# Zeroing the diagonal blocks of a decay attention's probabilities on GpSimd instead of adding a mask on TensorE

## What is computed

```python
scores = einsum('bhqd,bhkd->bhqk', q, k) / sqrt(8)
scores = where(causal, scores, -inf)
w = softmax(scores, axis=-1)
w = w * decay_weight_matrix(T)          # 1 near the diagonal, falling to 0
ctx = einsum('bhqk,bhkd->bhqd', w, v)
```

## Time and profile before

| | us |
|---|---|
| median of three runs | 5766.71 |
| lowest, highest | 5761.96, 5769.86 |
| the profiled execution, its own time | 5796.54 |
| its span | 5794.8 |
| first and last decay product on GpSimd (line 966) | start at 921.8 and 1410.1 |

### The profile page before, as it was taken

How to read it: one execution, slowest core, us unless ns; L and a number is a source line. 1 busy time by engine, 2 the same in 40 slices (tenths; PEclk the granted TensorE clock), 3 DMA queues, 4 the chain that set the end, 5 groups by cost and what they waited for, 6 DMA issues and landing times. The chain is left out here.

```text
span 5794.8 us, 91401 instructions
## 1 busy us (share of the span) xinstructions
PE 4718.3 (81%) x33501; PEld 2088.3 (36%) x33596; DVE 3782.7 (65%) x4596; ACT 3159.8 (55%) x6002; POOL 1685.3 (29%) x1468
## 2 busy tenths in 40 slices
PE   5677667998679977799766998589877799699999
PEld 2233223443233335333352333256432344233344
DVE  6899657886589943899437992577638710699410
ACT  5666444676448852488524885434466521388621
POOL 0666315885032324322242221000006400123100
PEclk7899888999889988899887999789989999799999
DMA  0000011111021124211242110000000000111100
GB/s 27 0 1 1 4 42 41 42 44 28 10 71 51 51 86 148 71 50 51 83 142 73 49 50 20 6 10 2 5 10 0 20 0 0 37 31 45 42 0 14
DMA packets 132106, 211.55 MB, mean 37 GB/s; under 512 B 36422, under 2 KB 93619, under 8 KB 130293
## 3 DMA queue, kind: packets, MB, share of 16 engines
q1 hardware_dynamic: 126708, 197.74, 11.3%
q0 software_dynamic: 4992, 8.41, 0.5%
HBM read 153.93 MB, written 52.00 MB: 36 GB/s over the span
## 5 line engine op out<-in xcount | busy, mean ns | idle before, releaser
L947 ACT ACTIVATE l_core_probs<-l_core_ps_scores_b 128x512 f32<-128x512 f32 (+3 forms) x3840 | 1610.7, 508 | 581.0 <-PE l_core_ps_scores_b L863 426.2
L1047 DVE TENSOR_REDUCE l_core_chunk_max<-l_core_ps_scores_a 128x2 f32<-128x1024 f32 (+3 forms) x1280 | 1253.7, 1021 | 82.9 <-PE l_core_ps_scores_a L848 47.8
L863 PE MATMUL l_core_ps_scores_b<-l_q_rows_sb,l_k_rows_sb 64*128 64x512 bf16 (+3 forms) x3840 | 944.0, 332 | 32.5 <-ACT l_core_probs L947 10.1
L848 PE MATMUL l_core_ps_scores_a<-l_k_rows_sb,l_q_rows_sb 64*128 64x512 bf16 (+3 forms) x3840 | 741.4, 346 | 163.9 <-DVE l_core_ps_acc L1005 75.9
L996 POOL TENSOR_SCALAR_AFFINE_SELECT l_core_probs<-l_core_probs 128x512 f32<-128x512 f32 x512 | 326.9, 639 | 1169.9 <-ACT l_core_probs L947 1165.7
L878 PE MATMUL l_core_ps_acc<-l_core_probs,l_v 128*9 128x512 f32 (+3 forms) x6144 | 648.9, 494 | 15.9 <-ACT l_core_out_sums L929 9.1
L1047 DVE TENSOR_REDUCE l_core_neg_max<-l_core_ps_scores_a 128x2 f32<-128x256 f32 (+3 forms) x640 | 493.6, 820 | 97.6 <-PE l_core_ps_scores_a L808 96.0
L863 PEld LDWEIGHTS l_core_ps_scores_b<-l_q_rows_sb,l_k_rows_sb 64*128 64x128 bf16 x3840 | 304.4, 94 | 689.9 <-ACT l_core_probs L947 600.4
L1918 POOL TENSOR_TENSOR l_scan_bx<-l_xs,l_scan_b_rows 128x1024 f32<-128x1024 f32 x192 | 452.5, 2357 | 224.1 <-DVE l_scan_states L1928 217.8
L1928 DVE TENSOR_TENSOR_SCAN l_scan_states<-l_scan_ps_decay,l_scan_bx 128x1024 f32<-128x1024 f32 x192 | 439.8, 2290 | 40.7 <-POOL l_scan_bx L1918 15.3
L966 POOL TENSOR_TENSOR l_core_probs_decayed<-l_core_probs,l_decay 128x1536 f32<-128x1536 f32 (+2 forms) x160 | 394.2, 2488 | 156.5 <-ACT l_core_probs L947 156.5
(11 more groups left out here) (323 smaller groups left out, 7683.4 us busy)
## 6 DMA issues: line engine op xcount, KB each, us to landing
l_slots_weights<-m_both_dram SPq DMA_DIRECT2D x78, 512.0 KB
l_q_rows<-l_proj_parts SPq DMA_DIRECT2D x96, 128.0 KB
l_k_rows<-l_proj_parts SPq DMA_DIRECT2D x96, 128.0 KB
l_q_rows_sb<-l_q_rows SPq DMA_DIRECT2D x128, 96.0 KB
l_k_rows_sb<-l_k_rows SPq DMA_DIRECT2D x128, 96.0 KB
l_heads_out<-l_core_out_sums SPq DMA_DIRECT2D x300, 32.0 KB
l_q_rows_sb<-l_q_rows SPq DMA_DIRECT2D x128, 64.0 KB
l_k_rows_sb<-l_k_rows SPq DMA_DIRECT2D x128, 64.0 KB
```

The costliest lines, as they stand in the source:

```text
L848: mm = nc.tensor.matmul(slot[:, i, 0:w], qs[n % 3][rows, p, qt * P:(qt + 1) * P], ks[n % 3][rows, p, c * NT:c * NT + w], start=True, stop= ...
L863: mm = nc.tensor.matmul(pb[m % 3][:, 0:w], ks[n % 3][rows, p, kt * P:(kt + 1) * P], qs[n % 3][rows, p, q0:q0 + w], start=True, stop=not diag)
L947: nc.scalar.activation(pt[:, ts % RP, j, 0:w], pb[m % 3][:, 0:w], ACT.Exp, scale=scale).then_inc(b_free, 1)
L1047: nc.vector.tensor_reduce(to, pa[e % 2][:, :, 0:width_a(qt, c)], AX.X, ALU.max, negate=True).then_inc(a_free, 1)
```

## The change

In the decay attention the second scores lose their mask products. Instead GpSimd runs the same `affine_select` as in the other layers on the four heads' diagonal blocks of `probs` (128 partitions by 4 x 128), ahead of the decay product of the same step, and the decay product waits for its end (`cut`). `values` on TensorE now waits for `cut` in this layer too. `PLAN_DECAY` is another string with the same counts. All else, the other attention layers too, stays.

```diff
-PLAN_DECAY = ("bbbvbaa", "bbvbba", "bvbabba", "babbb", "bbabavbaa", "bbvabba",
-              "bvbabbav", "bbabvab", "bbvabba", "bavbbbaav", "bbabab", "bvbbbaa")
+PLAN_DECAY = ("bbbvb", "bavbababa", "bvbbba", "bbabba", "babbvaab", "bbvbbaa",
+              "bbvbaba", "bvbbavb", "babvbb", "babbvb", "bbvbaaaaab", "bvbbbaaa")
...
-                    diag = decay and q0 == kt * P
...
-                    mm = nc.tensor.matmul(pb[m % 3][:, 0:w], ks[n % 3][rows, p, kt * P:(kt + 1) * P],
-                                          qs[n % 3][rows, p, q0:q0 + w], start=True, stop=not diag)
-                    if diag:
-                        mm = masked(pb[m % 3][:, 0:P], i, maskk, (slice(0, 64), slice(0, P)))
-                    mm.then_inc(b_ready, 1)
+                    nc.tensor.matmul(pb[m % 3][:, 0:w], ks[n % 3][rows, p, kt * P:(kt + 1) * P],
+                                     qs[n % 3][rows, p, q0:q0 + w], start=True, stop=True).then_inc(b_ready, 1)
...
-                    if not decay and on_diag(c, kt):
+                    if on_diag(c, kt):
                         pe.wait_ge(cut, had_diag(ts))
...
+                def cut_diagonal(ts):
+                    pool.wait_ge(b_free, 4 * ts + 4)
+                    block_ = pt[:, ts % RP, :, 0:P]
+                    nc.gpsimd.affine_select(block_, block_, [[0, 4], [1, P]], ALU.is_ge, none, base=0,
+                                            channel_multiplier=-1).then_inc(cut, 1)
+
                 if decay:
                     pool.wait_ge(c_in, CIN)
                     for ts in range(NS_ * GROUPS):
                         c, kt = STEPS[ts % NS_]
                         wd, off = decayed(c, kt), first_q(c, kt) - kt * P
+                        if on_diag(c, kt):
+                            cut_diagonal(ts)
+                            pool.wait_ge(cut, had_diag(ts))
                         if wd:
```

More of the change, by code:

```diff
@@ L956, in _ @@
             def _(pool):
+                none = nc.gpsimd.to_reg(0.0)
+                def cut_diagonal(ts):
[3 more added lines that the diff above has]
+                                            channel_multiplier=-1).then_inc(cut, 1)
                 if decay:
@@ L969, in _ @@
                 else:
-                    none = nc.gpsimd.to_reg(0.0)
                     def max_parts(n):
@@ L993, in _ @@
                         if on_diag(*STEPS[t]):
-                            pool.wait_ge(b_free, 4 * ts + 4)
-                            block_ = pt[:, ts % RP, :, 0:P]
-                            nc.gpsimd.affine_select(block_, block_, [[0, 4], [1, P]], ALU.is_ge, none, base=0,
-                                                    channel_multiplier=-1).then_inc(cut, 1)
+                            cut_diagonal(ts)
                         if t == 8 and n + 1 < GROUPS:
```

## The result

| | before | after |
|---|---|---|
| median of four runs, us | 5768.28 | 5873.31 |
| lowest, highest | 5761.96, 5771.29 | 5866.35, 5876.28 |
| the profiled execution's own time | 5796.54 | 5873.84 |
| one group of the decay core | 30.08 | 37.14 |

The ratio is 1.0182, with an interval of 1.0164 to 1.0199: the change makes the kernel 105 us slower. The stage itself accounts for it. From the first decay product to the end of the last `values` it runs from 921.77 to 1412.3 us before and from 921.73 to 1514.1 after, 101.8 us more. The 14 periods from the first step 7 to the fifteenth are 94.9 us of that (422.5 before, 517.4 after): most groups are 7.06 us longer, a few less. The remaining 7 us lie ahead of the first step 7 (2.4), between the last two (1.7) and at the end (2.7). I had said 5798, 5826 at most.

The account below looks back on a forecast made before the run. TensorE with its hand-overs set the pace before; after, a GpSimd loop of 32.15 us a group against 30.08 would: +29 over 14 periods, -1 as backlog drains, +2.8 at the end, together +31, 5798 us; range 5772 to 5826.

Parts of the forecast that it names:

- The direction: Whole kernel: slower by 31 us; slower given 81%, faster by more than 0.2% given 4%.
- the added work: GpSimd, decay core: eight selects a group at 0.70 us with hand-over, 5.6 us, raising its work from 24.47 to 30.1.
- the loop: GpSimd, step 3's `values`, ScalarE's copy, step 7: 28.8 + 3.35 = 32.15 us a group, +29 over 14 periods; 60%.
- the way back: From the end of step 3's decay product to step 7's start, through `values`, copy of `acc` and exponentials: 3.35 us.
- The end: Last five GpSimd products, alone on the path: four of these steps gain a select, +2.8 us.
- The term ahead of it: From the fifteenth step 7 to the last: GpSimd's backlog drains and the masks give back 1 us, -1.
- The price of the masks: TensorE's removed mask products in the second scores: 1.4 to 2 us a group, 22 to 32 if TensorE set the pace.
- VectorE's 26.63 fits too: VectorE's busy time of 26.63 us a group was taken to fit within the 32.15 us period.
- the order as a mere rival: The later turning of the maxima under the new plan was counted only in the shared-port rival, 17%, 5826 us.
- The second rival: Shared port and later turning: VectorE held for a GpSimd product, step 10 late 2 us; period 34.2, +59, 5826; 17%.
- The clock: TensorE's clock falls from waiting between steps 1 and 3, perhaps 2 us a group on the path: 5830; 5%.

Follow-up runs that it names:

- e1: The kernel after with the PLAN_DECAY order of before (selects, no mask products): 5837.36 us against 5797.98 before, ratio 1.0067, 32.43 us a group.
- e9: The kernel after with first-score units set where they stood before, second scores and `values` in the new order: 5802.37 us against 5764.12, 32.41 a group.
- e4: The kernel after with the old order and no selects, diagonal blocks left unmasked: 5788.79 us against 5797.98 before, ratio 0.9983, 29.49 a group.
- e12b: The kernel after with fourteen filler products on TensorE where its 4 us wait stands: 5859.89 us against 5765.00 before, 35.0 and 36.6 a group.
- e3: The kernel after with the remainder of VectorE's split of the maxima kept in PSUM: 5847.17 us against 5797.98 before, 32.13 or 33.7 a group.
- e11: The kernel before with the new order, masks kept, no selects, split remainder in PSUM: 5821.90 us against 5764.12 before, 33.15 or 34.8 a group.
- e6: The kernel before with only the split remainder moved to PSUM: 5772.89 us against 5764.12 before, ratio 1.0011, 30.08 us a group.
- e2: The kernel before with the new order alone, masks kept, no selects: 5890.60 us against 5797.98 before, ratio 1.0150, 35.9 to 37.1 a group.

## Why the prediction was wrong

**The direction and the added work were right.** Selects take 0.64 us, the hand-over to the product 0.07 to 0.08, and GpSimd's work a group rose to 29.5 (30.1 forecast, 29.6 without hand-over). GpSimd cannot take it in, for the reason given: e1 has the loop at 32.43 against 32.15. By itself this term gives e9's +38 us, where I had +31. In the kernel after the way back is 3.34 against 3.35, but that agreement is in part luck. One wait in it I had not named: step 6's product waits 0.64 us for the `values` of step 3, that is for a buffer. And I took 3.35 instead of 3.75 because one more unit of step 7 stands ahead. e9 has that unit ahead too, and its way back is 3.65 (1000.65 to 1004.30); the last 0.3 came with the new places of the first-score units.

**The end was right.** From step 7's product of the last group to the last product's end pass 16.76 us after (1496.68 to 1513.44) and 14.10 before: 2.66 more, 2.8 forecast. The term ahead of it was not: from the fifteenth step 7 to the last I had -1 us, since the backlog would drain; measured are 38.41 us after and 36.71 before, +1.7.

**The price of the masks was too high**, 0.59 us a group measured by e4 and 1.4 to 2 forecast from the earlier trace rows. I priced TensorE's rate where TensorE is only one of the engines that pass the work around. It did not matter for the sum, which GpSimd's loop set. Two small slips did not matter either: the lower bounds of my terms add up to 31.0 us, not 31.3, and ahead of step 10 stand two selects, not three (10.55 us behind step 7, where I wrote 10.7; 10.54 in e1).

**The step that failed** is "VectorE's 26.63 fits too", and with it the order as a mere rival. I compared each engine's sum with the period, and the sums do fit: e1 runs with 27.59 us of VectorE in 32.43. But the change puts the turning six second-score units later, with three first-score units in a row behind it, and there are two buffers of first scores. In that bunch the two engines can only take turns, and step 10's last unit stands behind it in the queue. e9 against the kernel after gives the price of those places: 4.7 us a group, two thirds of the loss.

**The second rival had this mechanism and was mis-sized.** It named VectorE held for a whole GpSimd product (3.4 us; 3.50 measured), the unit behind it and GpSimd's step 10 that waits. It set the period at 34.2 by being 2 us late. Measured at full clock it is 35.0 (e12b). The lateness at step 10 was nearly right: GpSimd waits 1.82 us there in e12b. Left out were the units behind it, by which step 0 is late too (0.95), and the clock.

**The clock was put apart as a rare case (5%), and it is a consequence.** A block of 3.4 us on VectorE, which the second rival had, leaves TensorE about as long without work at its third first-score unit; 4.02 us were measured. The earlier trace rows showed what follows such a stretch: 0.57 for four microseconds. The two had to be taken together: 34.2 and some 2 us of clock would have been 36.2, and 5855 us.

**How the 4.7 us divide.** 2.1 are the clock (37.14 less e12b's 35.0) and 2.9 the block and what waits behind it (35.0 less e3's 32.13). That is 0.3 too much, and the 0.3 is the shorter way back of the new places: 3.35 us in e3, 3.65 in e9. The split holds on top of the selects only; without them e11 leaves 3.1 us to the bunch itself.

**What stays open.** Why the clock falls in e3, e11 and e12b in some groups and not in others, at waits that look alike, was not settled; nor why the last but one group grew by 1.7 us. The profiled execution of before was 29.8 us over its median and I expected the same of the one after, which was not (5873.84 against a median of 5873.31): the former looks to be from one of the chips that measure 5798, by the 4040 us of its layers behind the stage.

## What to carry to other kernels

Busy sums say whether an engine can keep up over a group, not whether it can at a place: where an order puts several small units of one kind in a row between two engines with two buffers, walk through the queue there, and ask what stands behind the last of them. Work added to an engine with room is free only if its idle time is where the work is; close the loop (which of its results does it wait for, by which queue?) and count the period from that. And take linked effects together: where a rival makes TensorE wait for several microseconds, look for a place in the trace where it waited like that, and put the clock that followed there into the same sum.

## What the runs showed of the hardware

A VectorE operation of 0.2 to 0.3 us on 32x128 numbers in SBUF took 3.50 us, the length of the GpSimd product that had begun just before it. A cast from SBUF to SBUF (2.84 us in e9) and a subtraction of two SBUF operands (3.50 us) were both caught. The same operations with an input in PSUM were not (0.28 us each in e3). Being free of it is worth between nothing (e6) and 2.9 us a group, by what waits.

The Trainium skill (SBUF — State Buffer, Who interferes with whom) has this rule: VectorE and GpSimd share a port pair, for which casts and copies in a two-port mode and operations with two SBUF inputs contend, and one with at most one SBUF input outside those modes does not. The traces agree.

TensorE's clock went from full to half inside a wait of 4.02 us, and came back within 6 us in which the engine was almost always busy (0.50 from 1063.2 to 1068, 1.00 from 1069). It fell around a wait of 2.52 us too (e2), and in some groups of e3 behind three waits of 0.3 to 0.8 us; in e9 it stayed full at waits of 1.48 and 1.17. Fourteen products without a use in the wait kept it full in half of the groups (e12b).
